# Graph layer on one core: 32-node windows per quarter, z tiles in two halves of the array, gathered rows added to z by TensorE

## What is computed

```
msg_in     = [h[src](64), h[dst](64), ef(32)]
messages   = silu(msg_in @ W1  + b1 ) @ W2  + b2
att_logits = silu(msg_in @ Wa1 + ba1) @ Wa2 + ba2    # softmax over all edges
aggregated = segment_sum(messages * softmax(att_logits), dst, 6250)
out        = x + silu([h, aggregated] @ Wu1 + bu1) @ Wu2 + bu2
```

## Time and profile before

| | us |
|---|---|
| median of 3 runs | 2454.44 (2444.82 to 2455.82) |
| span of the profiled execution | 2482.0 |
| POOL busy | 1529.9 (62%) |
| PE busy, its weight loads | 1101.1 (44%), 963.4 (39%) |
| DVE busy | 1086.6 (44%) |
| ACT busy | 919.5 (37%) |
| mean granted TensorE clock | 0.668 of full speed |
| DMA | 228.43 MB, mean 92 GB/s |

### The profile page before, as it was taken

How to read it: one execution, slowest core, us unless ns; L and a number is a source line. 1 busy time by engine, 2 the same in 40 slices (tenths; PEclk the granted TensorE clock), 3 DMA queues, 4 the chain that set the end, 5 groups by cost and what they waited for, 6 DMA issues and landing times.

```text
span 2482.0 us, 21022 instructions
## 1 busy us (share of the span) xinstructions
PE 1101.1 (44%) x6767; PEld 963.4 (39%) x6767; DVE 1086.6 (44%) x2367; ACT 919.5 (37%) x1107; POOL 1529.9 (62%) x1628
## 2 busy tenths in 40 slices
PE   4334444444444444444444444444444444444447
PEld 3223343444333333444333334343433333444444
DVE  4344444444444444444444444444444444444445
ACT  3333333334333333334333333343433333333433
POOL 4666666666666666666666666666666666666650
PEclk8566666666666666666666666666666666666766
DMA  7433333333333333333333333333333333333321
GB/s 202 106 90 90 90 89 88 92 91 95 98 93 88 90 88 88 90 93 90 99 95 89 89 90 89 87 94 89 98 95 91 89 90 90 87 93 90 95 65 27
DMA packets 101990, 228.43 MB, mean 92 GB/s; under 512 B 45184, under 2 KB 65460, under 8 KB 91636
## 3 DMA queue, kind: packets, MB, share of 16 engines
q1 hardware_dynamic: 47588, 120.63, 18.5%
q0 software_dynamic: 51584, 105.75, 17.2%
q10 hardware_dynamic: 2704, 0.66, 0.1%
HBM read 218.91 MB, written 8.00 MB: 91 GB/s over the span
## 4 chain that ended last, share of the span: by engine, by line
issue 48%; PE 33%; DVE 9%; another core or an unknown queue 7%; ACT 1%; SPq 1%; DVEq 0%; DMA 0%; ACTq 0%
PE bank L622 20%; PE bank L636 11%; DVE hot L865 2%; DVE v L902 2%; DVE bank L912 1%; DVE prod L895 1%; PE bank L732 1%; PE bank L722 0%; DVE lgb L921 0%; DVEq L875 0%; ACT comb L492 0%; PE bank L584 0%; ACT s L524 0%; PE bank L655 0%
## 5 line engine op out<-in xcount | busy, mean ns | idle before, releaser
L404 POOL DMA_INDIRECT p_rows<-p_tab,src_all x1612 | 1521.9, 944 | 872.3 <-issue 464.7
L622 PE MATMUL bank<-q_win,comb 128*128 128x128 f32 x3224 | 723.7, 369 | 981.9 <-issue 963.8
L622 PEld LDWEIGHTS bank<-q_win,comb 128*128 128x128 f32 x3224 | 643.9, 279 | 1099.1 <-issue 1095.4
L492 ACT ACTIVATE comb<-dst_b,row_of 96x1024 f32<-96x1024 int32 (+1 forms) x162 | 219.0, 1352 | 1336.6 <-PE bank L622 1227.8
L911 DVE TENSOR_TENSOR bank<-bank,p_rows 128x128 f32<-128x128 f32 x80 | 23.9, 299 | 1205.5 <-remote 672.6
L636 PE MATMUL bank<-hot,v 128*65 128x96 f32 x3200 | 320.1, 252 | 344.7 <-issue 274.8
L636 PEld LDWEIGHTS bank<-hot,v 128*65 128x65 f32 x3200 | 282.7, 141 | 342.1 <-issue 264.5
L912 DVE TENSOR_TENSOR bank<-bank,p_rows 128x512 f32<-128x512 f32 (+1 forms) x403 | 266.5, 666 | 71.7 <-PE bank L622 38.6
L524 ACT ACTIVATE s<-bank 128x512 f32<-128x512 f32 x403 | 232.1, 589 | 108.7 <-DVE bank L912 83.8
L498 ACT ACTIVATE comb<-comb,ones 96x1024 f32<-96x1024 f32 (+1 forms) x162 | 218.9, 1351 | 2.7
L865 DVE TENSOR_TENSOR hot<-bank,rel 128x960 f32<-128x960 f32 x162 | 178.3, 1139 | 0.0
(11 more groups left out here) (108 smaller groups left out, 304.0 us busy)
## 6 DMA issues: line engine op xcount, KB each, us to landing
dst_b<-dst_row SPq DMA_DIRECT2D x80, 960.0 KB
p_rows<-p_tab,src_all POOLq DMA_INDIRECT x1612
comb<-efT SPq DMA_DIRECT2D x80, 320.0 KB
q_win<-q_tab SPq DMA_DIRECT2D x81, 48.0 KB
p_tab<-s SPq DMA_DIRECT2D x12, 256.0 KB
q_tab<-s SPq DMA_DIRECT2D x12, 256.0 KB
out<-s SPq DMA_DIRECT2D x6, 256.0 KB, 2.3
x_sb<-x SPq DMA_DIRECT2D x2, 512.0 KB, 5.1
```

The costliest lines, as they stand in the source:

```text
L404: pool.indirect_dma_start(p_rows[:, a, t * H2:(t + 1) * H2], None, p_tab, bass.IndirectOffsetOnAxis(src_all[:, g * TG + t:g * TG + t + 1], ...
L492: nc.scalar.activation(comb[0:WIN, a, c0:c1], dst_b[:, c0:c1], ACT.Abs, bias=row_of[0:WIN, bass.ds(g, 1)]).then_inc(abs_ok, 1)
L622: last = nc.tensor.matmul(ps_z[q][:, (t % TQ) * H2:(t % TQ + 1) * H2], comb[:, a, t * P:(t + 1) * P], q_win[:, a, :], start=True, stop=True)
```

## The change

- Windows: each quarter has its own window of 32 nodes (QW) instead of one of 96 nodes for each group. `comb` and `q_win` are laid out in two halves of 64 partitions, each 32 one-hot rows and 32 feature rows. Tiles 0, 1 of a quarter lie in one half, tiles 2, 3 in the other; a tile's matmul has contraction 64, and the two halves' matmuls alternate.
- PE adds the gathered rows: two matmuls for each quarter with `ident` as weights and 256 columns of `p_rows`, accumulating on z. `add_rows` is gone from DVE. POOL now waits for `z_done`.
- z has three slots of two banks, taken in turn; PE does z of its own group g (quarters 0, 1, 2, then `sums(g-1)`, then 3, 4) instead of the next one.
- The one-hot is one DVE comparison for each group (`own_nodes`) instead of four ACT passes.
- SP loads 10 pieces of window for each group, two of features, two of `dst_b` (32 partitions each, half the columns).

```diff
-            node = eng.value_load(base_i[0:1, bass.ds(g, 1)], min_val=0, max_val=N - WIN)
-            eng.dma_start(q_win[0:WIN, a, :], q_tab[bass.ds(node, WIN), :]).then_inc(win_ld[a], 16)
+            for q in range(quarters(g)):
+                node = eng.value_load(bases_i[0:1, bass.ds(NG + g * NQ + q, 1)], min_val=0, max_val=N - QW)
+                for h in range(2):
+                    eng.dma_start(q_win[h * HB:h * HB + QW, a, q, :], q_tab[bass.ds(node, QW), :]).then_inc(win_ld[a], 16)
...
                 nxt2 = following(g)[1]
                 if nxt2 is not None:
-                    sp.wait_ge(abs_ok, 2 * g + 4)
-                    load_dst_b(sp, nxt2)
                     sp.wait_ge(z_done, (g + 1) * NQ)
+                    load_windows(sp, nxt2, a)
+                    sp.wait_ge(own_ok, g + 3)
+                    if nxt2 < LAST:
+                        load_dst_b(sp, nxt2 + 1)
                     load_ef(sp, nxt2, a, ef_ld[a])
-                    load_window(sp, nxt2, a)
...
                     if g > 1:
-                        if q == 3:
-                            pool.wait_ge(tile_ok, g - 1)
-                        else:
-                            pool.wait_ge(z_ok, (g - 2) * NQ + q + 1)
+                        pool.wait_ge(z_done, (g - 2) * NQ + q + 1)
...
-                wait(pe, silu_ok, (g - 1) * NQ + q + 1)
-                if q in (0, 2):
-                    pe.wait_ge(comb_ok, 2 * g + 1 + q // 2)
-                for t in range(q * TQ, (q + 1) * TQ):
-                    last = nc.tensor.matmul(ps_z[q][:, (t % TQ) * H2:(t % TQ + 1) * H2], comb[:, a, t * P:(t + 1) * P], q_win[:, a, :],
-                                            start=True, stop=True)
+                wait(pe, silu_ok, g * NQ + q + 1 - SLOTS)
+                out = slot(g, q)
+                for k in range(TQ // 2):
+                    for h in range(2):
+                        rows_h, cols = slice(h * HB, (h + 1) * HB), slice(q * QH + k * P, q * QH + (k + 1) * P)
+                        nc.tensor.matmul(out[:, h, k * H2:(k + 1) * H2], comb[rows_h, a, cols], q_win[rows_h, a, q, :], start=(k == 0), stop=False)
+                pe.wait_ge(gath[a][q], per(a, g, 16 * TQ))
+                for h in range(2):
+                    t = q * TQ + 2 * h
+                    last = nc.tensor.matmul(out[:, h, :], ident[:], p_rows[:, a, t * H2:(t + 2) * H2], start=False, stop=True)
                 last.then_inc(z_done, 1)
...
             def group(g, a):
-                nxt = following(g)[0]
-                late = not (isinstance(g, int) and g == 0)
-                quarters = range(tiles(nxt) // TQ) if nxt is not None else []
-                for q in [q for q in (0,) if q in quarters]:
-                    zmm(nxt, 1 - a, q)
-                for q in [q for q in (1, 2) if q in quarters]:
-                    zmm(nxt, 1 - a, q)
-                if late:
-                    sums(g - 1)
-                for q in [q for q in (3, 4) if q in quarters]:
-                    zmm(nxt, 1 - a, q)
+                for q in range(quarters(g)):
+                    if q == 3 and g > 0:
+                        sums(g - 1)
+                    zmm(g, a, q)
...
+            def own_nodes(g, a):
+
+                n = quarters(g)
+                nc.vector.tensor_scalar(node_no[:, a, 0:n], base[:, NG + g * NQ:NG + g * NQ + n], row_in[:, 1:2], None, ALU.subtract).then_inc(node_ok, 1)
+                dve.wait_ge(node_ok, g + 1)
+                dve.wait_ge(dst_b_ld, 32 * (g + 1))
+                wait(dve, z_done, (g - 1) * NQ)
+                nc.vector.tensor_tensor(comb[:, a, 0:n * QH].rearrange("p (q e) -> p q e", e=QH), dst_b[:, 0:n * QH].rearrange("p (q e) -> p q e", e=QH),
+                                        node_no[:, a, 0:n].unsqueeze(2).broadcast_to([P, n, QH]), ALU.is_equal).then_inc(own_ok, 1)
...
                 if late:
                     one_hots(g - 1, 0)
                     one_hots(g - 1, 1)
                     weighted(g - 1, 1 - a)
-                if g == LAST - 1:
-                    add_rows(g, a, 3)
-                    add_rows(g, a, 4)
+                if following(g)[1] is not None:
+                    own_nodes(g + 2, a)
```

More of the change, by code:

```diff
@@ L22 @@
 EDGE_TILES = 20
+TILE = 128
 F32 = mybir.dt.float32
@@ L46, in build @@
     DUP = C - E
-    WIN = P - DE
+    WIN = 96
+    QW = DE
+    HB = 2 * QW
+    NQT = C // (TQ * P)
+    QH = TQ // 2 * P
+    GH = NQ * QH
+    SLOTS = 3
     NT = -(-N // P)
@@ L257, in tiles, with quarters, slot, windows_landed @@
             return TL if is_last(g) else TG
+        def quarters(g):
+            return tiles(g) // TQ
+        def slot(g, q):
+            return z[:, (g * NQ + q) % SLOTS, :, 0:QH]
+        def windows_landed(g):
+            return 32 * (NQ * (g // 2) + quarters(g))
         def per(a, g, n):
@@ L300, in _ @@
             sp.dma_start(x_sb[0:LT, NT - 1, :], x[(NT - 1) * P:N, :]).then_inc(x_ld[2], 16)
-            with nc.allow_non_contiguous_dma(reason="one dst of each group"):
-                sp.dma_start(first_i[:, 0:LAST], dst_row[:, 0:LAST * GE].rearrange("a (g e) -> a g e", e=GE)[:, :, 0]).then_inc(first_ld, 16)
-            sp.dma_start(first_i[:, LAST:NG], dst_row[:, LAST * GE:LAST * GE + 1]).then_inc(first_ld, 16)
+            with nc.allow_non_contiguous_dma(reason="one dst of each quarter"):
+                sp.dma_start(first_i[:], dst_h[0:1, :].rearrange("a (q e) -> a q e", e=QH)[:, :, 0]).then_inc(first_ld, 16)
             sp.dma_start(src_all[:, 0:TG], src[:, 0:TG]).then_inc(src_ld[0], 16)
@@ L596, in _ @@
                     pe.wait_ge(base_ok, 1)
-                    nc.tensor.matmul(ps_small[:, 0:NG], ones[0:1, :], base_f[:], start=True, stop=True).then_inc(baseB_done, 1)
+                    nc.tensor.matmul(ps_small[:, 0:NG + NQT], ones[0:1, :], bases_f[:], start=True, stop=True).then_inc(baseB_done, 1)
             for b in range(NB + 1):
@@ L654, in own_part @@
                 wait(pe, su_ok, b - 5)
-                nc.tensor.matmul(ps_u[b][0:rows_of(b), 0:n], wu1d[:, 0:rows_of(b)], hP[:, b * UT // 2 * P:b * UT // 2 * P + n], start=True, stop=False)
-            for q in range(NQ):
-                zmm(0, 0, q)
+                nc.tensor.matmul(ps_u[b][0:rows_of(b), 0:n], wu1d[:, 0:rows_of(b)], hP[:, b * UT // 2 * P:b * UT // 2 * P + n], start=True, stop=True)
             groups(pe, group)
-            pe.wait_ge(silu_ok, (LAST - 1) * NQ + 5)
-            own_part(0)
-            own_part(1)
-            pe.wait_ge(silu_ok, LAST * NQ + TL // TQ)
-            for b in range(2, 5):
-                own_part(b)
+            sums(LAST - 1)
+            for q in range(TL // TQ):
+                pe.wait_ge(silu_ok, LAST * NQ + q + 1)
+                own_part(2 * q)
+                own_part(2 * q + 1)
             pe.wait_ge(acc_ok, LAST)
```

216 lines of the change are left out of this document (98 added, 118 removed).

## The result

| | before | after |
|---|---|---|
| median of 4 runs, us | 2455.13 | 3129.2 (3120.26 to 3140.2) |
| ratio, 95% interval | | 1.2765 [1.2724, 1.2806] |
| span of the profiled execution, us | 2482.0 | 3118.5 |

Slower, as forecast, but by 27% instead of 5%: 3129 lies far outside the range of 2340 to 2800. The nearest case was the rival with two long waits (2951, chance 0.12).

The account below looks back on a forecast made before the run. No engine full; POOL's gathers 1986.6, start 40.0, waits 376.4 and end 79.1 made 2482.1 us. Adding 105 (wait), 7 (start), 10 (end) gave 2604, less 28: about 2575 us, + 4.9%; range 2340 to 2800.

Parts of the forecast that it names:

- the rival with two long waits: POOL stops at quarter 2 and again at quarter 3; waits 10.8 us in all, 2951 us; chance 0.12.
- What bounds the kernel: POOL's gathers keep number and pace, 1986.6 us; start, end and POOL's waits of 376.4 us decide.
- It decides if a quarter costs PE 2 us at full clock, so that z2 ends 9 us or more after the restart.: PE's z of quarter 2: the limit at which the case of two long waits a group would come.
- So z2 ends 7.0 us after POOL's restart. POOL has its five quarters.: PE's loop: z3 3.0 us, z4 2.5, z0 to z2 1.5 each, letting POOL run five quarters.
- `v` comes at about 14 us: DVE's chain: begins at z4, 2.5 us after the restart, and takes 11.7 us to `v`.
- The wait: POOL's wait for z, once a group at quarter 3: 6.0 us instead of 4.66, + 105 us.
- The 70 instructions ahead: PE can issue about 70 instructions ahead of what is seen, then needs 0.96 us for each.
- a quarter of z: PE's work for one quarter: 2.5 to 3.4 us, taken as 3.0 at 1.2 GHz and 1.5 at 2.4 GHz.
- the comparison: DVE's one-hot comparison over 1280 columns: 1.5 us, with a small one 1.7.
- first gather of group 2: Start of the kernel: first gather of group 2 at about 105, from 104.7 against 97.5, + 7 us.
- the end: After POOL's last gather: two groups of about 16 to 17 us each instead of 11.7, + 10 us.
- Half-depth steps: PE's eight half-contraction steps of a quarter: 1.7 us without overlap of the halves, 0.85 with full overlap.

Follow-up runs that it names:

- e13: Kernel with weights behind silu of quarter 0, plus features and receivers loaded ahead of windows and `hot` and `v` built ahead of the next logits: 2596.51 us, 1.0583.
- the first pause: Changed kernel plus a POOL scratch fill and wait, about 1.3 us, before the gathers of quarter 0 of each group: 2751.91 us, 1.1214.
- the second, where the chain no longer hung on the late completion: Same pause before quarter 0's gathers, added to the kernel with weights behind silu of quarter 0: 2579.03 us, 1.0515.

## Why the prediction was right in its direction and wrong in its size

- **What bounds the kernel** was right: the gathers' pace didn't move (945 ns each), and POOL's waits carry 647.6 us. That the slowness comes with the gathers as POOL issues them is shown by the two runs with plain transfers, and that their unbroken order matters by the pause that made the changed kernel faster; that it is their being indirect is not shown by itself.
- **The step that failed: "It decides if a quarter costs PE 2 us at full clock, so that z2 ends 9 us or more after the restart."** The forecast's own loop rests on that limit: "So z2 ends 7.0 us after POOL's restart. POOL has its five quarters." z2 ended 6.5 us after it, at 1.7 us a quarter (forecast 1.5), but was seen 16 us later, so POOL had four. In the kernel that had z2 at 3.1 us, and in the group opened of the one that had it at 4.6, POOL did not stop for it. I had put the limit at 9 us without a row for it: the earlier trace rows show PE getting 68 instructions done 40 us into a run, which says how far it can issue, not when a completion is seen.
- **"`v` comes at about 14 us"** failed with it. The sum counted VectorE's work and forgot ScalarE's order: the weights stand behind silu of quarter 2. `v` ended 29.5 us after the restart. With the weights freed from it, the changed kernel takes 2475. Where z2 was seen 1.1 us behind its end, in the run without identity matmuls, `v` ended at 13 us, close to the 14 forecast.
- **The wait** was 3.2 + 10.0 = 13.2 us a group, not 6.0. The rival of two waits had the right places and 10.8 us; its second wait counted sums and z3 but not exp, `hot` and `v` (5 us) ahead of them, and had 4.5 us of sums where the row shows 6.00.
- **"The 70 instructions ahead"** is partly right: 64 went at speed in one run, 52 in another, 80 in a third. It doesn't set the time: halving the sums gave 1.4% in the kernel before where 3 to 4% was expected, though 6% in e13.
- **Right in size:** a quarter of z 3.16 us at 1.2 GHz, its identity steps 0.50 each there (forecast 0.42) and 0.26 at 2.4 GHz; the comparison 1.49 us; first gather of group 2 at 103.4 (forecast 105); the end 90.7 us (forecast 89); `dst_b` cleared at no cost that can be told (first gather at 40.9, before 40.0).
- **Half-depth steps.** The first quarter of group 0 (start, us), and windows with the granted clock (third value from the end): 0.50 for 3.1 us behind an idle time of 35 us, then 1.00.

```profile
99.89 1.23 PE L621 MATMUL z<-q_win,comb 64*128 64x128 f32 x8 [35.07 <-DMA comb<-ef_h]
101.05 2.07 PE L625 MATMUL z<-p_rows,ident 128*128 128x256 f32 x4
```

```profile
99.90:103.00 3.10, 3.10 (x12) 2.09 (x12) 0.08 (x1) 0.00 (x0) 0.00 (x0) 0.50 0.08 22
103.40:108.00 4.60, 4.60 (x36) 3.27 (x32) 1.51 (x3) 1.55 (x3) 3.68 (x4) 1.00 0.55 131
```

From 99.89 to 101.05 are eight steps, 0.145 us apart, against 0.212 at full depth and a clock of 0.55: 1.5 times as fast, 1.6 with the clocks counted. The eight steps took 1.16 us, between the prediction's 0.85 and 1.7. The Trainium skill (TensorEngine Tiling, Theoretical Speedup) allows up to 2x, and the row stays under it. The drain at a change of mode that the Trainium skill names (TensorEngine Tiling, Key Properties) can't be told apart in these rows.

What stays open: why the stops sum to 4.5 to 4.8 us per 20 gathers in six quite different schedules (before; before with a pause, this counted in; weights at quarter 0; at quarter 1; `v` first; features first with half of the sums). It isn't a floor: the kernel before with half of the sums stops 4.1 us. Open too is what in the run of gathers holds TensorE's completions back, its indirect transfers, their number or its having no break, and whether the matmuls or only their signals are late.

## What to carry to other kernels

Where one engine issues indirect gathers without a pause, look for waits released by nothing near them ("remote"), and ask of each of TensorE's completions in the loop whether it falls early enough in the run to be seen; put nothing in an in-order queue behind one that isn't. A dependency's price is set by what stands behind it in its queue: one edit to ScalarE's order was worth 654 us of 674. A short pause, work added, is a cheap test of whether a stall is visibility or work: here the first pause made the kernel 377 us faster, while the second, where the chain no longer hung on the late completion, only cost its time.

## What the runs showed of the hardware

- **Late completions differ between chips.** The kernel before took 2453 to 2486 us on all chips but one, and 2107 on that. 2107 is about what the gathers alone give: 2482.0 - 376.4 = 2106 us. On that chip silu started 0.04 us behind z in the middle of an unbroken run; on the others up to 16 us behind. Half of the sums, worth 1.4% in the kernel before on one of the others, is worth 0.0% on it.
- **How late depends on how long the run of gathers has gone.** In the changed kernel, over 77 groups, a z that ended 1.4 or 3.1 us after a restart was seen 0.04 us later in every group; one at 4.8 us 0.04 to 7.9 us later (4.4 in the middle), one at 6.5 us 15.3 to 16.2. It is no sharp rule: at 3.1 us, with all five quarters ending in those 3.1 us, the fifth was seen 1.1 us late or more, and in another kernel z's at 1.6 and 3.8 us were seen 1.3 and 3.4 us late, one at 4.6 us 13.8.
- **A stop** for something long done lasted (beyond the usual gap of 0.30, in the middle of its groups) 1.0 us behind 4 gathers, 1.9 behind 8 that followed a pause, 2.5 behind 12 and 2.9 to 3.1 behind 16.
- **VectorE's and ScalarE's completions are not late.** In the run with the weights at quarter 0, TensorE's sums start 0.05 or 0.06 us behind `v` in 79 of 79 groups, though `v` ends 15.8 us after a restart in the middle of them. In the changed kernel VectorE starts on its logits 0.03 us behind silu in all 60 cases in which it waited for a silu that ended over 8 us after a restart.
- **SyncE's issuing is slowed with TensorE's**: ten window loads took 20.35 us beside gathers, 12.75 in the run with the pause, 6.92 at the start while POOL was stopped; on the other chip 6.92 beside gathers too.
